# A mixture-of-experts loop with computed jumps: the first expert's turns leave the expert programs and get a choice and leaves of their own

## The reference, cut to what matters

```python
top_v, top_i = jax.lax.top_k(logits, K)
...
kept = pos < C                                    # C = 1280 slots of an expert
slot = jnp.where(kept, experts * C + pos, E * C)
buf = jnp.zeros((E * C + 1, D), x.dtype).at[slot].set(xf[tokens])
xb = buf[:E * C].reshape(E, C, D)
gu = jnp.einsum('ecd,efd->ecf', xb, w12)
g, u = jnp.split(gu, 2, axis=-1)
h = jax.nn.silu(g) * u
yb = jnp.einsum('ecf,edf->ecd', h, w3).reshape(E * C, D)
ys = yb[jnp.minimum(slot, E * C - 1)] * (weights * kept.astype(weights.dtype))[:, None]
out = jnp.zeros((T, D), x.dtype).at[tokens].add(ys)
```

## Time and profile before

| | us |
|---|---|
| median of 3 runs (2670.05 to 2671.79) | 2671.38 |
| the profiled execution's own time | 2672.94 |
| its span, first to last instruction | 2671.2 |
| TensorE matmul busy | 2599.4 (97%) |
| TensorE weight load busy | 2313.1 (87%) |
| VectorE busy | 1362.1 (51%) |
| ScalarE busy | 952.6 (36%) |
| the expert loop, from the first comparison (487.8) to the end of the span | 2183.4 |

### The profile page before, as it was taken

One profiled execution on the slowest core, in us unless ns is written; L12 is line 12 of the kernel. 1 busy time (PEld: TensorE's weight loads), 2 busy tenths in 40 slices (PEclk: granted clock), 3 DMA queues, 4 the chain that ended last, 5 costly groups with the idle time before them and its releaser, 6 DMA issues.

```text
span 2671.2 us, 40600 instructions
## 1 busy us (share of the span) xinstructions
PE 2599.4 (97%) x14168; PEld 2313.1 (87%) x14169; DVE 1362.1 (51%) x2628; ACT 952.6 (36%) x2498; POOL 422.7 (16%) x399
## 2 busy tenths in 40 slices
PE   7999999699999999999999999999999999999998
PEld 6888887699998888889888788888888999989987
DVE  5888887444444444454444444444434444445555
ACT  6777776222223222232222322322223322233343
POOL 5556565200001000010000200100001100030030
PEclk9999999799999999999999999999999999999999
DMA  8422323321114011140110511221013211142142
GB/s 332 176 97 91 107 80 112 121 88 47 47 36 110 28 43 47 34 116 24 47 47 27 124 48 71 68 71 48 24 47 71 77 47 47 47 90 102 71 128 82
DMA packets 58994, 208.37 MB, mean 78 GB/s; under 512 B 8517, under 2 KB 8797, under 8 KB 50563
## 3 DMA queue, kind: packets, MB, share of 16 engines
q1 hardware_dynamic: 42242, 175.30, 18.2%
q0 software_dynamic: 16640, 31.69, 6.2%
HBM read 145.60 MB, written 67.70 MB: 80 GB/s over the span
## 4 chain that ended last, share of the span: by engine, by line
PE 88%; DVE 4%; issue 3%; ACT 2%; POOL 1%; DMA 1%; another core or an unknown queue 1%; DVEq 0%; SPq 0%; ACTq 0%; POOLq 0%
PE bank L1601 78%; PE bank L947 6%; ACT staged L493 1%; PE bank L1047 1%; PE bank L1607 1%; PE bank L1011 1%; PE bank L1022 1%; DVE before L828 1%; PE bank L1038 0%; DVE neg_max L703 0%; POOL expert_rows L422 0%; POOL staged L389 0%; DVE xT_lo L640 0%; DVE yacc L1541 0%
## 5 line engine op out<-in xcount | busy, mean ns | idle before, releaser
L1561 DVE TENSOR_TENSOR h<-silu,bank 128x384 f32<-128x384 f32 (+2 forms) x320 | 183.8, 574 | 828.0 <-PE bank L1601 818.3
L1601 PE MATMUL bank<-slotsT_hi,early_hi 128*128 128x384 f32 (+2 forms) x1280 | 445.9, 348 | 13.1 <-issue 11.6
L1601 PE MATMUL bank<-slotsT_hi,w_hi 128*128 128x384 f32 (+2 forms) x1280 | 442.3, 346 | 3.2 <-DVE w_lo L1502 3.2
L1601 PE MATMUL bank<-slotsT_hi,early_lo 128*128 128x384 f32 (+2 forms) x1280 | 443.0, 346 | 1.7 <-issue 1.7
L1601 PE MATMUL bank<-slotsT_lo,early_hi 128*128 128x384 f32 (+2 forms) x1280 | 443.5, 346 | 0.0
L1601 PE MATMUL bank<-slotsT_lo,w_hi 128*128 128x384 f32 (+2 forms) x1280 | 442.1, 345 | 0.0
L1601 PE MATMUL bank<-slotsT_hi,w_lo 128*128 128x384 f32 (+2 forms) x1280 | 440.9, 344 | 0.0
L1469 ACT CAST h_hi<-h 128x384 fp32r<-128x384 f32 (+2 forms) x320 | 169.2, 529 | 744.0 <-DVE h L1561 741.1
L1463 ACT ACTIVATE silu<-bank 128x384 f32<-128x384 f32 (+2 forms) x320 | 162.0, 506 | 725.6 <-PE bank L1601 725.0
L1411 POOL DMA_INDIRECT out_dram<-yout,token x63 | 97.9, 1554 | 1969.4 <-ACT yout L1455 1957.9
L1541 DVE TENSOR_TENSOR yacc<-bank,yacc 128x512 f32<-128x512 f32 x464 | 316.6, 688 | 168.8 <-PE bank L1601 167.9
(11 more groups left out here) (199 smaller groups left out, 3508.9 us busy)
## 6 DMA issues: line engine op xcount, KB each, us to landing
staged<-in_moe_w_dram SPq DMA_DIRECT2D x33, 1536.0 KB
raw<-in_moe_w_dram SPq DMA_DIRECT2D x32, 1536.0 KB
xrow<-expert_rows SPq DMA_DIRECT2D x42, 520.0 KB, 8.8
expert_rows<-zeros SPq DMA_DIRECT2D x40, 520.0 KB, 7.8
xin<-in_x_dram SPq DMA_DIRECT2D x17, 512.0 KB, 3.8
xres<-in_x_dram SPq DMA_DIRECT2D x15, 512.0 KB, 3.7
out_dram<-xres SPq DMA_DIRECT2D x15, 512.0 KB
staged<-in_L_xattn_Wq_dram SPq DMA_DIRECT2D x1, 1024.0 KB, 7.2
```

The source lines that it names most:

```text
L1561: nc.vector.tensor_tensor(h32[q % 2][:, 0:W], silu[q % 2][:, 0:W], UB[q % 2][:, 0:W], ALU.mult)\
L1601: last = nc.tensor.matmul(out_ap, st, mv, start=(at == 0), stop=(at == n - 1))
```

## The change

The opening leaves the programs. The top gets a first comparison of its own (is this the first expert?). Behind it stands a choice for the first expert alone, whose eight leaves each hold a hint, the opening, and a jump to the program, to which the hint points; then, behind these leaves, a second choice for all later experts, which jumps to the programs; then the eight programs, 10 tiles first, without `If` and without opening.

```diff
                     def whole(nt):
-                        with eng.If(e < 1):
-                            opening()
                         chunk(nt, e, 0, 0, 0, True, False)
...
+                    def opened(nt):
+                        here = eng.mark_branch_hint_location()
+                        opening()
+                        late = f"{name}_{nt}_late"
+                        eng.br_lt(index, E, on_true=f"{name}_{nt}", on_false=late).branch_hint(here)
+                        with nc.body(late, valid_engines=mine):
+                            nc.br(f"{name}_{nt}", engines=mine)
+
-                    def pick(sizes):
+                    def pick(sizes, first):
 
                         if len(sizes) == 1:
-                            whole(sizes[0])
+                            if first:
+                                opened(sizes[0])
+                            else:
+                                nc.br(f"{name}_{sizes[0]}", engines=mine)
                             return
-                        more = f"{name}_over_{sizes[0]}"
-                        eng.br_lt(n_e, sizes[0] * P + 1, on_true=f"{name}_{sizes[0]}", on_false=more)
+                        more = f"{name}_{first}_over_{sizes[0]}"
+                        chosen = f"{name}_{sizes[0]}_opening" if first else f"{name}_{sizes[0]}"
+                        eng.br_lt(n_e, sizes[0] * P + 1, on_true=chosen, on_false=more)
                         with nc.body(more, valid_engines=mine):
-                            pick(sizes[1:])
-
-                    pick(TILES)
-                    for nt in reversed(TILES[:-1]):
+                            pick(sizes[1:], first)
+
+                    opens, later = f"{name}_opens", f"{name}_later"
+                    eng.br_lt(index, 1, on_true=opens, on_false=later)
+                    with nc.body(opens, valid_engines=mine):
+                        pick(TILES, True)
+                    for nt in TILES[:-1]:
+                        with nc.body(f"{name}_{nt}_opening", valid_engines=mine):
+                            opened(nt)
+                    with nc.body(later, valid_engines=mine):
+                        pick(TILES, False)
+                    for nt in reversed(TILES):
                         with nc.body(f"{name}_{nt}", valid_engines=mine):
                             whole(nt)
```

## The result

| | before | after |
|---|---|---|
| median of the four runs compared, us | 2671.28 | 2697.84 (2696.01 to 2699.04) |
| ratio, 95% interval | | 1.010 (1.008 to 1.012) |
| profiled execution, its span, us | 2671.2 | 2695.6 |
| granted clock, mean | 0.987 | 0.984 |

The change costs 26.6 us. The forecast was 2701.4 us, 30.0 us more. These are the parts of the changed kernel's page that answer to the earlier trace rows: span, busy time by engine, and the queues with which TensorE (q8) and ScalarE and VectorE (q14) fetch code.

The account below looks back on a forecast made before the run. TensorE, busy 97% of the span, was taken as the bound, so only stops count, priced by code fetches. Terms for experts 0 to 7 and the clock sum to 30.0 us: 2671.38 becomes 2701.4 us, range 2680 to 2712.

Parts of the forecast that it names:

- B: TensorE's code block right behind the top's block; the second choice would lie in it and it would be refetched.
- Item 1: Second choice lies in B, fetched in 3.40 us; TensorE stands still 1.8 us at experts 1, 2, 4 and 5.
- Out at all seven passes: Claim that B is out of TensorE's instruction memory each time a later expert, 1 to 7, needs it.
- My walk: Count through TensorE's blocks in order of last use: eight blocks or more always ran since B's last use.
- Item 2: Expert 3 on TensorE: waits for B, then misses its program, but saves the opening's 3.40 us branch; +0.7 us.
- Item 3: Expert 5 on TensorE: its 1.74 us stop goes, the second choice costs 1.8, some stop may stay; +0.5 us.
- Item 4: Expert 6 on TensorE: B's wait adds 3.0 us, and a block border gives a second stop; +6 us.
- Item 6: Expert 0 on TensorE: leaf's hint void, jump to the program after the turns fetches for 3.7 to 4.65 us; +2.
- ScalarE's delay: ScalarE loses top and second choice, about 5.5 us late at experts 1, 4, 6, 7; +6, +6, hidden, +5.5.
- Item 7: Granted clock: stops at experts 1 and 4 would add stretches at low clock; +1.5 us (0 to 5).
- TensorE alone: Rival: only TensorE is late, ScalarE keeps its top and second choice; 14.9 us more, 2686 us; chance 0.22.

Follow-up runs that it names:

- the early hint: The changed kernel with the hint for each program's jump back to the top set ahead of the inner loop instead of the last chunk; ratio 1.0064, about 17 us slower than before.
- the single engines: Three kernels, each with only one engine's loop in the changed form, the others as before; ratios 1.0060 for TensorE, 1.0072 for ScalarE, 0.9999 for VectorE.

## Why the prediction was right, and where its terms were off

The direction, the mechanism and the sum held: 30.0 forecast, 26.6 by the medians and 28.0 by the traces. The step behind it all was that top and 10-tile program now lie on nine blocks where eight fit. From 1132 to 1480 us q8 lists ten packets, nine of them between expert 2's passes through the top, one for each block; with the leaves moved behind the programs expert 2 lists none. The Trainium skill ("Runtime: NRT & Kernel Launch", section "Instruction fetch mechanics") calls this memory a FIFO, and says that a taken branch to a target outside "the current 2-page window" forces a fetch. The rows disagree with such a window: the kernel before ran expert 2, the top and a program of seven blocks with a jump back across them, without one packet, so the measurement decides for a memory that keeps eight blocks for reuse.

Which block goes for a new one stays open. The prediction says what was used longest ago, and its own count does not bear that out. Expert 3 had left two of the old eight blocks, and by that rule expert 4's fetch of B pushes out the older of the two, which is then fetched again: seven blocks behind the top, as many as expert 1 fetched (807 to 1143). Expert 4, with the same program, fetched six (1727 to 2063).

- *Item 1, the second choice:* 3.1 to 3.5 us a time, forecast 3.40; 1.5 us net at experts 1 and 2, forecast 1.8. Shown. "Out at all seven passes" was wrong for expert 7: line 1344 took 0.22 us. By the four packets on q8 behind its first block, the 5-tile program before it took five blocks; with the top, the choice's block and the one behind it, that is eight. In the kernel without the leaf's hint it took one more, and expert 7 missed the block (3.94 us). My walk had counted one block too many.
- *Item 2, expert 3:* +0.7 forecast, +0.6.
- *Item 3, expert 5:* +0.5 forecast, +2.3, just above my upper end of 2. The stop at the border was still there, 1.67 us, ahead of the last of 8 transposes: 12 products and 7 turns are 38 of the 42 instructions that I had put between start and border. I had let 42 instructions hide the fetch; they run for 3 us. Three packets on q8 start at 2082.1, 2085.6 and 2088.5; I read them as the choice's block, the one behind it and the one behind the border, which so came last. The trace doesn't say what a packet holds.
- *Item 4, expert 6:* 6 forecast, 3.6. The jump's 5.84 us came as said, the second stop did not. It came when the programs lay 8 instructions nearer, and the program then took a block more. So in the changed kernel it starts at most 8 instructions behind a border, where I had put it ten ahead of one: this term failed by the place, and it takes the place to a few instructions to tell.
- *Item 6, expert 0:* 2 forecast, 3.8. The leaf's hint was void as said, but the jump took 6.33, above my 3.7 to 4.65. The jump began at 495.8 and its packet started only at 499.6; at expert 6 that took 1.8 us. No other code was fetched ahead of it, as q8 lists nothing from 487 to 499.5. The DMA engines moved 444 GB/s in those 3.8 us, and 138 GB/s at expert 6's, but that this held the packet back is not shown.
- *ScalarE:* its tops were lost at experts 1, 4, 6 and 7 and at no other, each 3.8 to 5.4 us, and the second choice took 2.2 to 3.4 more, where I had at most 1.7. Expert 1 cost 7.9 and not 6 for that. At expert 7 I had 5.5 us and it was 2.1: TensorE's wait for the weights' low part grew from 3.2 to 5.4 us, and with ScalarE's top found (the early hint) it was 3.3 again. So ScalarE's delay moved it, but by 2.2 of its 6.6 us. I had taken the delay in full; the rest was probably slack, as VectorE's own top was over 4 us late in both kernels.
- *Item 7, the clock:* forecast 1.5; it is at most the 3.0 us by which the measured growth exceeds the new idle time. The 30 us around expert 1's start show it (granted clock third from last), where the kernel before has 1.00 from 805 to 835 us:

```profile
805.00:835.00 30.00, 23.81 (x116) 0.94 0.47 92
```

So experts 6 and 7, together 5.8 us too much, were made up for by experts 0, 1 and 5, together 5.5 too little: the sum is better than its terms, and that is luck. The rivals are told apart by the single engines: TensorE alone is real and costs about what that rival said (14.9 forecast, 16 by the ratio, 17.5 by the trace), and ScalarE's share comes on top.

## What to carry to other kernels

Where sequencers jump among programs, count code in fetch blocks: what one iteration touches, the dispatch included, has to fit the memory, and code used once belongs behind the code that is used again. In these kernels a hint worked only where it stood in another block than its jump; check it by the time from jump to target, not by how early it is. Near a block border a few instructions decide on a stop of 1.4 to 3.4 us, so a shift that "changes nothing" has to be measured.

## What was not expected of the hardware

- Single-engine versions of the change cost 16 and 19 us, and together 26.6: the delays of late engines overlap.
- A hint 10.3 us ahead of its jump was void in the same block, one 6.3 us ahead worked across a border.
- A jump into missing code took from 1.8 to 6.7 us in these kernels, in the changed kernel 3.1 to 3.5 us into the block behind the top's and 4.0 to 6.3 us elsewhere. What makes the longest ones long is open.
- Removing eight instructions elsewhere made experts 6 and 7 together 5 us slower.
